# Ranking by source in the weighted sum: a predicated copy replaced by a product with the mask and an addition

## The reference, cut to what matters

```python
src = src[_o]; dst = dst[_o]          # sorted by dst
...
x_j = x[edge_index[0]]
msg = norm[:, None] * x_j
agg = jax.ops.segment_sum(msg, edge_index[1], num_segments=x.shape[0])
return jax.nn.relu(agg @ W + b)
```

## Time and profile before

| | us |
|---|---|
| median of 3 runs | 22322.45 (22279.1 to 22326.45) |
| the profiled execution | 22313.08 |
| its span, first to last instruction | 22311.4 |

### The profile page before, as it was taken

The page is one execution under the profiler, slowest core; times in us unless marked ns, Lnnn a source line. Parts: engine busy times, 40 slices in busy tenths (PEclk is TensorE's granted clock), DMA queues, the critical chain, the costliest instruction groups (busy, mean ns, idle before and its releaser), DMA issues. The chain is left out here.

```text
span 22311.4 us, 374370 instructions
## 1 busy us (share of the span) xinstructions
PE 13477.0 (60%) x78008; PEld 11646.6 (52%) x78009; DVE 14663.0 (66%) x38171; ACT 8055.3 (36%) x18940; POOL 11007.6 (49%) x11458
## 2 busy tenths in 40 slices
PE   0333333323333333336999778888887888888887
PEld 0223332223333333336999645555556777777776
DVE  2167772112222222225888689999998999999999
ACT  5622222211000000001222157767774555555554
POOL 0677776664666666663111100000003777777776
PEclk9555555555555555557999789999998888888888
DMA  1111111112222222222333233323332222222223
GB/s 55 14 15 15 15 15 15 14 14 27 58 57 58 58 58 58 58 58 41 34 34 33 22 99 102 102 87 103 103 102 56 43 43 43 43 43 43 43 43 40
DMA packets 2941218, 1095.84 MB, mean 49 GB/s; under 512 B 2415654, under 2 KB 2635015, under 8 KB 2940041
## 3 DMA queue, kind: packets, MB, share of 16 engines
q1 hardware_dynamic: 2278776, 643.54, 14.8%
q0 software_dynamic: 312576, 231.97, 6.4%
q10 hardware_dynamic: 349748, 219.11, 3.7%
HBM read 999.36 MB, written 98.48 MB: 49 GB/s over the span
## 5 line engine op out<-in xcount | busy, mean ns | idle before, releaser
L2698 POOL DMA_INDIRECT conv_far<-conv_rows x3232 | 3066.1, 949 | 2925.0 <-DMA weighted_far<-in_x_dram,weighted_rows 2076.5
L794 POOL DMA_INDIRECT weighted_far<-in_x_dram,weighted_rows x3232 | 3331.0, 1031 | 1983.9 <-issue 1053.1
L1546 POOL DMA_INDIRECT rows_by_src<-push_row,push_index x3232 | 3152.0, 975 | 1704.2 <-issue 1577.6
L1323 DVE TENSOR_SCALAR hop_hots<-hop_wide_iota,hop_nodes 128x512 bf16<-128x512 f16 x11904 | 3544.3, 549 | 2.9 <-PE hop_sums_ps L1396 2.8
L878 PE MATMUL weighted_total<-weighted_message,weighted_hot 128*128 128x33 f32 x6464 | 1513.9, 404 | 3345.1 <-issue 1811.8
L1620 PE MATMUL push_near<-far_rows_sb,push_turned 128*128 x6464 | 1677.4, 434 | 2902.7 <-issue 2027.3
L878 PEld LDWEIGHTS weighted_total<-weighted_message,weighted_hot 128*128 128x128 f32 x6464 | 1428.0, 329 | 3431.7 <-issue 3431.2
L1396 PE MATMUL hop_sums_ps<-hop_hots,place_i 128*96 128x512 bf16 x11904 | 2827.9, 380 | 494.8 <-DVE hop_hots L1323 376.6
L2804 PE MATMUL conv_radial_a<-radial,conv_hidden 128*128 128x256 f32 x6464 | 2738.0, 511 | 640.3 <-DVE conv_products_b L2936 565.5
L1620 PEld LDWEIGHTS push_near<-far_rows_sb,push_turned 128*128 128x128 f32 x6464 | 1576.0, 328 | 2949.5 <-issue 2948.6
L1579 DVE TENSOR_TENSOR push_place<-push_place,push_trash 128x4 f32<-128x4 f32 x808 | 132.6, 164 | 3489.1 <-DMA push_place<-place_by_dst 3158.9
(11 more groups left out here) (345 smaller groups left out, 27025.3 us busy)
## 6 DMA issues: line engine op xcount, KB each, us to landing
hop_line<-sources_of_tiles SPq DMA_DIRECT2D x744, 512.0 KB
push_line<-local_by_group ACTq DMA_DIRECT2D x808, 256.0 KB
conv_weights<-weight_by_group SPq DMA_DIRECT2D x808, 128.0 KB
att_far<-rows_by_src SPq DMA_DIRECT2D x880, 80.0 KB
weighted_far<-in_x_dram,weighted_rows POOLq DMA_INDIRECT x3232
push_place<-place_by_dst SPq DMA_DIRECT2D x3232, 0.5 KB
rows_by_src<-push_row,push_index POOLq DMA_INDIRECT x3232
conv_rows<-edges_by_dst SPq DMA_DIRECT2D x3232, 4.0 KB
```

The lines of the kernel that those rows point to most:

```text
L794: pool.indirect_dma_start(far[s][:, j, :], None, table, bass.IndirectOffsetOnAxis(ap=rows[s][:, j, 0:1].bitcast(I32), axis=0)).then_inc(ga ...
L1323: last = dve.tensor_scalar(hot[lot % HOTS][:, j, :], wide_iota[:], nodes[s][:, half * LOT_TILES + j:half * LOT_TILES + j + 1], None, ALU.i ...
L1546: pool.indirect_dma_start(k.rows_by_src, bass.IndirectOffsetOnAxis(ap=index[s][:, j:j + 1], axis=0), row[s][:, j, :], None).then_inc(writt ...
L2698: pool.indirect_dma_start(far[s][:, j, :], None, k.conv_dram, bass.IndirectOffsetOnAxis(ap=rows[s][:, j, 0:1].bitcast(I32), axis=0)).then_ ...
```

## The change

Each bin's ranking gets a fourth operation. `mask_ranks`, in slot 2 of each half turn, multiplies `q.running` in place by `q.mine`, so that it is zero outside the bin; `keep_places`, in slot 3 as before, adds `q.running` to `q.place`. As each edge is in exactly one bin and `q.place` starts at zero, the sum over all bins is the place of every edge. Both call sites are changed, the one in the turns of `weighted_sum` and `place_bin`. Line numbers behind L511 are 7 to 9 higher in the changed kernel.

```diff
@@ -505,16 +505,23 @@
+def mask_ranks(dve, s, q):
+
+    s.wait()
+    s.step(dve.tensor_tensor(q.running[:], q.running[:], q.mine[:], ALU.mult))
+
+
 def keep_places(dve, s, q):
 
     s.wait()
-    s.step(dve.copy_predicated(q.place[:], q.mine[:], q.running[:]))
+    s.step(dve.tensor_tensor(q.place[:], q.place[:], q.running[:], ALU.add))
 
 
 def place_bin(dve, s, k, q, b):
 
     mark_bin(dve, s, q, k.iota[:, bass.ds(b, 1)])
     rank_bin(dve, s, k.ones[:, 0:1], q, q.first[:, bass.ds(b, 1)])
+    mask_ranks(dve, s, q)
     keep_places(dve, s, q)
     s.wait()
@@ -835,6 +842,8 @@
                             mark_bin(dve, sort, q, iota[:, bass.ds(at, 1)])
                         elif step == 1:
                             rank_bin(dve, sort, iota[:, 1:2], q, q.first[:, bass.ds(at, 1)])
+                        elif step == 2:
+                            mask_ranks(dve, sort, q)
                         elif step == SLOTS - 1:
                             keep_places(dve, sort, q)
                             sort.wait()
```

## The result

| | before | changed |
|---|---|---|
| median, us | 22322.3 | 22528.03 |
| runs, us | 22279.1 to 22326.45 (4) | 22502.06 to 22546.45 (4) |
| ratio | | 1.0094, interval 1.0082 to 1.0106 |
| profiled execution, us | 22313.08 | 22546.45 |

The change makes the kernel 206 us slower by the medians, 233 us by the two profiled executions. The forecast was 22497 us, in a range of 22435 to 22620, and the measured median lies in it.

What follows compares the result with a forecast made beforehand. POOL's gathers were taken to bound the ranking. Holds rising from 2.78 to 2.57 + 2.40 us a bin over 98 bins add 215 us; 40 us less row waiting leaves +175, giving 22497 us, range 22435 to 22620.

Steps and rivals of the forecast that it cites:

- The bound: In the ranking stretch, POOL's gathers, their holds and row waits set the turn of 46.9 us; DVE's work is hidden.
- What holds a gather: In the ranking, a gather begun during a DVE operation with both inputs in SBUF waits until about 0.8 us after its end.
- the two operations of the table and the short one: Two-SBUF-input operations before the change: two while the table is made held gathers to 3.50 and 2.83 us, a 0.56 us one a scatter.
- The product's hold: In each of 98 bins of the source ranking, the new product holds POOL for 2.57 us.
- u: Time from a DVE operation's start to POOL's next gather start; 0.70 us for the copy, used for the product too.
- The addition's hold: In each ranking bin, the new addition holds POOL for 2.40 us, taken between 2.08 and 2.57.
- both conditions occur: At the addition, DVE is sometimes behind (hold 2.08 us) and sometimes caught up (2.57 us), hence 2.40.
- The waits for rows: In the ranking, POOL's 54.1 us of waiting for edge rows mostly goes as turns lengthen; 40 us taken back.
- The sum: Over 98 ranking bins, holds rise from 2.78 to 4.97 us, +215 us; less 40 us of row waits, net +175 us.
- (1): Rival for the ranking: product and addition do not stop POOL, so 272 us leave its path, 22050 to 22380 us; chance 0.07.
- (2): Rival for the ranking: only one new operation holds, the addition mostly falling where POOL waits anyway; -20 us, 22303; chance 0.06.
- Rival 3: In the ranking, holds add up fully and DVE falls behind, masks late for PE; +370 us or more, 22690; chance 0.10.

## Why the prediction was right, point by point

- **The bound.** That POOL's issue of gathers sets the ranking's pace, and not DVE, was right: the product with its ones in PSUM loads DVE to 89% and costs nothing, and the time of every kernel run follows POOL's holds.
- **What holds a gather.** That the product and the addition hold gathers as the copy does, taken from the two operations of the table and the short one, was right, and is now shown by the exchange of one operand (+272 us from SBUF, -5 from PSUM, all else equal). Of the two rules of the Trainium skill (SBUF — State Buffer, "Who interferes with whom"), the one that lets a DVE instruction with two SBUF inputs contend with a GpSimd instruction that reads SBUF agrees with this case's traces (a gather of 3.16 us beside the product with both inputs in SBUF, gathers of 0.94 us beside the one with its second input in PSUM); the inference that a `tensor_tensor` leaves descriptor generation alone does not hold for these gathers.
- **The product's hold.** 2.57 us was forecast, and the 98 held gathers give 2.67 on average: 0.10 us more, 10 us in all. The mean u, taken from the copy as 0.70 us, was 0.61 here. The copy's hold, 2.78 by the prediction, is 2.78 one by one as well.
- **The addition's hold: the term that was mis-sized.** "If DVE is behind, it starts 1.15 us after the product's end, as the marking does behind the copy" was wrong. Behind the copy there is a wait on its end, behind the product there is none, so the addition comes 0.78 us after it, ahead of POOL's next gather, with u = 0.34 and a hold of 2.94 us instead of the 2.40 taken. Nor did "both conditions occur": all 98 additions start 0.77 to 0.79 us after the product's end, with u from 0.33 to 0.35. That is +0.54 x 98 = +53 us. Putting the wait there gave the 2.07 that the forecast had as its lower end.
- **The waits for rows.** 40 of 54.1 us were taken back; 49.0 went (5.1 left in the same 2200 us). On the other chips there is little of it to save: the product with ones in PSUM, as fast there as the kernel before, waits 1.5 us for rows from 1250 to 3050, where the kernel before on the first chip waits 42.2. There the change costs 259 us instead of 206.
- **The sum.** Forecast +175, measured +206 by medians: +53 for the addition, +10 for the product and -9 for the waits make +229, against +233 between the profiled executions and 223 by the start of the ranking's last operation. So the sum closes with these terms. The forecast was low by the one term, and the range had room for it because it reached further up than down.
- **The rivals.** The holds did not vanish (1), and neither fell where POOL waits anyway (2): 196 of 196 operations hold a gather. Rival 3 was partly right: the addition's hold of 2.94 us lies nearer to its largest value of 3.27 than to the 2.40 taken. But late masks did not set the pace: POOL's wait for rows, through which they would reach it, was 5.1 us in 2200.
- **What would show it.** About 196 held gathers of 2.8 to 4.3 us were forecast (196, of 3.02 to 4.13). Forecast were a mean gather of 1.26 us (1.306), a turn near 50.5 (51.5), the last operation near 3650 us (3696): each off in the same direction, mostly by the addition's hold.

## What to carry to other kernels

These runs show it for one kernel, with gathers of 0.94 us and one DVE operation of about 3.5 us at a time. When POOL issues indirect transfers and they set the pace, look in the timeline for transfers much longer than the rest, and at what DVE runs beside them. Then two remedies are worth a try. A long operation with all inputs in SBUF can be cut into pieces of about the length of one gather's own time or less (here 391 columns, 0.58 us: -1.1%). Or one of its inputs can be put in PSUM, which costs DVE nothing where that input is a repeated column (3.40 us either way); a full-width input in PSUM was not tried. Count such operations, and where they start relative to POOL's next instruction, rather than DVE's microseconds.

## What the runs showed that was not expected

- A wait more on DVE made the kernel 72 us faster, because it moved the next holding operation by 0.37 us to just behind the start of a gather.
- A gather is held by one piece only: DVE's next piece starts before the one ahead has ended (five pieces of 0.80 us take 3.68 us, not 4.0), and still the held gather gets through between them.
- The chips differ: the kernel before takes 22322 us on one and 21120 on the others. In counting, the former issues 326 gathers in 500 us and the latter 375 or 376, at the same 944 ns for a gather, so its rows come later: POOL waits 73.6 us for them in the kernel before on the first chip, 29.7 in the changed kernel on another. Why they do was not tried, and the kernels in pieces were not run on the slower chip: there, up to the 7.4 us a turn for which POOL waits for rows outside the ranking may take back part of their gain.
